# A two-layer transformer kernel: the Linear layer's products grouped by row count, LN2's steps of batch 0 placed half a unit earlier, the first sides' fills on ScalarE

## Chip, cores, metric

One NeuronCore of a Trainium2 chip. The metric is the time of one execution on the device in microseconds (us), taken as the median of several runs; lower is better. The engines are named PE (TensorE), DVE (VectorE), ACT (ScalarE), POOL (GpSimd) and SP (SyncE, which issues the transfers).

## What is computed

x has 2 batches of 1024 tokens with 128 features. Four sublayers follow one another, each on the layer-normalised x and added to x:

```
x = x + _L0_attn_ref(_layernorm(x), ...)   # causal attention, 16 heads of 64, scores/8, softmax/8
x = x + _L0_ffn_ref(_layernorm(x), ...)    # Linear layer with a gated low-rank part
x = x + _L1_attn_ref(_layernorm(x), ...)   # attention by squared distances, 16 heads of 8
x = x + _L1_ffn_ref(_layernorm(x), ...)    # 1 shared and 8 gated experts, 128 -> 512 -> 128, silu

# _L0_ffn_ref, the sublayer that the first part of the change touches
base = jnp.einsum('bcd,od->bco', x, W)
l = jnp.stack([... x @ Wd_i.T @ Wu_i.T for ranks 1, 2, 4, 8 ...], axis=2)
res = jnp.sum(ret[..., None] * l, axis=2)      # ret: the gate of the one chosen rank
return base + res

# _L1_attn_ref
Q = x @ W_k.T
scores = -(|q|^2 - 2 q.k + |k|^2) / sqrt(8)
attn_out = softmax(scores) @ Q @ merged, then @ W_o.T
```

All of it is in float32.

## The kernel before

The program is written engine by engine, and each engine runs its instructions in the written order. Semaphores join them; nothing is scheduled by a tool. All activations stay in SBUF: `x` and `xn` by token tiles of 128 (`[128, 16, 128]`), `xT` by features. PSUM is one tensor `banks` of eight banks of 512 columns.

**The first attention** runs in 16 units, u = 0 to 15, each one pair of heads of one batch (units 0 to 7 batch 0, 8 to 15 batch 1). `units0` calls `unit0_pe`, `unit0_act`, `unit0_dve` and `unit0_pool`. A unit has ten slots, handled two by two in five groups i = 0 to 4. In each slot PE makes a score block (`scores_pe`, L455 to L461), ACT takes its exp (`exp_act`, L603), POOL masks it where the diagonal is in it (L860) and adds it into `pacc` for the row sums (L868 for the first block of a half, L871 for the others), and PE multiplies it with the values (`pv_pe`, L481). In the same unit PE and DVE prepare the next one (n = u + 1): max products (`max_pe`, L406), row maxima by DVE (`max_dve`, L726 and L731), projections (L339) and their rounded and residual parts (ACT L608, DVE L710). `sums_pe` (L489) sums the rows of `pacc`, ACT takes logarithm and exp (L632, L634), DVE makes a Newton step (`newton_dve`, L739, L741) and `z_dve` (L752), and `out_pe` (L500) projects unit u - 1, which `xacc_dve` (L758) adds to x.

**Later sublayers of batch 0 are fitted into units 8 to 15**, by `if u == ...` lines in these functions: LN1 in units 8 to 10, the router in 11 and 12, in unit 13 at i = 1 the Linear layer (`linear_mid_pe`, L1127 base product with 128 rows, L1128 low-rank product with 16 rows, eight tiles of each in two halves, one bank for a half; `x_mid_dve`, L1135, adds it to x). LN2 follows: `stats_mid_dve` (L948) at i = 3 of unit 13, `aggr_mid_dve` (L952) and `eps_mid_dve` (L956) at i = 4, `rstd_mid_act` (L961, L963) at i = 4, `newton_mid` (L969 to L975) on POOL at slot 0 of unit 14, `norm_mid_dve` (L980, eight tiles) at i = 0 of unit 14, and at i = 1 PE's transposes (`turn_mid_pe`, L992), which wait for the normalised tiles and for the third maximum of n = 15, because they reuse its banks. Maxima, normalising and all else on DVE are in one queue.

**In unit 15** the first of the eight units of the second attention is set up: `heads1_pe` (L1200), `merged_pe`, `proj1_pe` and `norm1_pe` (L1211, L1217) at i = 0 and 1, into banks 6 and 7. From them `sides1_dve` makes the two matrices of the distance product: for each half of 512 columns a rounded copy (L1243), two fills (L1246) and two additions (L1250). `s_rl` counts the last two kinds. `out_pe` of unit 14 at i = 3 of unit 15 uses bank 7 and waits for `s_rl` 8, that is for all sides. `merged_wo_pe` (L1168) at i = 4 uses bank 6 and waits for `s_rl` 4. DVE's `newton_dve(u, 0)` and `xacc_dve(u - 1)` stand at i = 3.

**The second attention** (`attn1_pe`, and the same for the other engines) has 8 units of 32 blocks: a distance product (L1278), exp on ACT (`exp1_act`, L1305), products with the values (L1292). The Linear layer of batch 1 is fitted into its third unit, in four parts of two tiles. The experts come last.

## Time and profile before

| | |
|---|---|
| three runs | 1069.88, 1070.07, 1075.11 us |
| median | 1070.07 us |
| the profiled execution, its own time | 1073.41 us |
| its span, first to last instruction | 1071.7 us |
| its mean granted PE clock | 0.971 of full |
| first attention, with its start | to about 557 us |
| second attention | about 557 to 820 us |
| experts, with the last layer norm and router | about 820 us to the end |

The page gives busy time by engine and the largest groups of instructions; the timeline gives instructions in order of time, merged where they are alike, with the idle time before them and what ended it. An fp32 matmul appears as two instructions. Starts and waits are exact; the ends of matmuls are modelled, so durations of stages are read here from start to start.

### The profile page before, as it was taken

The numbers are of one execution on the slowest core, as the hardware profiler recorded it, in microseconds if no ns is written. First come the engines' busy times: TensorE is split into PE (matmuls) and PEld (weight loads), VectorE is DVE, ScalarE is ACT, GpSimd is POOL, SyncE is SP. The second block draws the span as 40 slices with busy tenths as digits, with TensorE's granted clock in tenths as the row PEclk, the third lists the DMA queues.
The fourth block names the chain that finished last, engine by engine and source line by source line (L and its number), as shares of the span: only waits on it lengthen the run. The fifth ranks groups of instructions, "written<-read, shape, count | busy, mean of one in ns | idle before, by whom it ended". The sixth has DMA issues, their size and how long they took to land.

```text
span 1071.7 us, 18837 instructions
## 1 busy us (share of the span) xinstructions
PE 1002.6 (94%) x6927; PEld 591.6 (55%) x6927; DVE 718.7 (67%) x1481; ACT 698.5 (65%) x1019; POOL 561.5 (52%) x504
## 2 busy tenths in 40 slices
PE   4789999999999999998989999999996599999997
PEld 3546666666666666665643333333222377877785
DVE  5767777777778768757555434434212699999998
ACT  3346666666566666635548998899996576666564
POOL 3267877787777768844860000000000258887885
PEclk9699999999999999988999999999999699999999
DMA  2000000000000000200000010000000003121201
GB/s 96 8 9 8 1 9 9 8 9 9 9 9 10 1 9 9 59 1 1 2 3 7 9 14 10 11 10 9 13 11 11 1 2 120 71 87 59 78 40 39
DMA packets 24927, 23.52 MB, mean 22 GB/s; under 512 B 17612, under 2 KB 20316, under 8 KB 23820
## 3 DMA queue, kind: packets, MB, share of 16 engines
q1 hardware_dynamic: 24844, 22.42, 7.4%
q8 instruction: 52, 0.85, 0.3%
q14 instruction: 31, 0.25, 0.1%
HBM read 19.20 MB, written 1.11 MB: 19 GB/s over the span
## 4 chain that ended last, share of the span: by engine, by line
PE 65%; DVE 20%; issue 9%; ACT 3%; SPq 1%; DMA 1%; DVEq 0%; ACTq 0%
PE banks L481 11%; PE banks L1292 10%; PE banks L1278 6%; DVE big L1699 5%; PE banks L339 4%; PE banks L406 4%; PE banks L455 4%; PE banks L500 3%; PE banks L461 3%; PE banks L489 3%; PE banks L459 3%; PE banks L457 3%; PE banks L432 3%; ACT prob L603 1%; PE banks L1211 1%
## 5 line engine op out<-in xcount | busy, mean ns | idle before, releaser
L871 POOL TENSOR_TENSOR pacc<-pacc,prob 128x1024 f32<-128x1024 f32 (+3 forms) x160 | 274.8, 1717 | 82.9 <-ACT prob L603 71.4
L1305 ACT ACTIVATE prob<-banks 128x1024 f32<-128x1024 f32 x256 | 240.4, 1068 | 20.8 <-PE banks L1278 19.5
L603 ACT ACTIVATE prob<-banks 128x1024 f32<-128x1024 f32 (+1 forms) x160 | 150.1, 940 | 150.0 <-PE banks L461 145.4
L1732 POOL TENSOR_TENSOR big<-prob,big 128x512 fp32r<-128x512 f32 x108 | 165.1, 1549 | 59.3 <-ACT big L1682 32.5
L481 PE MATMUL banks<-prob,v 128*64 128x512 f32 (+3 forms) x768 | 146.3, 503 | 0.0
L1688 ACT ACTIVATE prob<-banks,w 128x512 f32<-128x512 f32 x144 | 94.4, 685 | 70.9 <-PE banks L1650 70.8
L1292 PE MATMUL banks<-prob,v 128*32 128x512 f32 x1024 | 136.2, 604 | 1.2 <-DVE pacc L1313 1.0
L1225 POOL TENSOR_TENSOR wqkv<-wqkv 64x512 f32<-64x512 f32 x8 | 8.3, 1033 | 197.9 <-DVE wqkv L1221 197.9
L1670 PE MATMUL banks<-big 128*128 128x512 f32 x432 | 106.6, 392 | 4.5 <-POOL big L1732 4.5
L1650 PE MATMUL banks<-big 128*128 128x512 f32 x432 | 106.2, 394 | 1.3 <-ACT prob L1688 1.3
L1278 PE MATMUL banks<-big 32*128 32x512 f32 x512 | 100.8, 503 | 0.8 <-ACT prob L1305 0.8
L726 DVE TENSOR_REDUCE mxa<-banks 128x2 f32<-128x1024 f32 x64 | 77.0, 1222 | 31.7 <-PE banks L406 31.0
L1278 PEld LDWEIGHTS banks<-big 32*128 32x128 f32 x512 | 43.2, 181 | 94.6 <-ACT prob L1305 61.3
L1670 PEld LDWEIGHTS banks<-big 128*128 128x128 f32 x432 | 80.2, 188 | 24.7 <-POOL big L1732 5.6
L1650 PEld LDWEIGHTS banks<-big 128*128 128x128 f32 x432 | 81.8, 190 | 20.0 <-ACT prob L1688 2.1
L731 DVE CUSTOM_DVE_ANT_0 banks<-banks,msk,mxa 128x128 f32<-128x128 f32 (+3 forms) x128 | 65.7, 556 | 39.0 <-PE banks L406 38.3
L860 POOL TENSOR_SCALAR_AFFINE_SELECT prob<-prob 128x256 f32<-128x256 f32 x128 | 50.6, 408 | 74.2 <-ACT prob L603 74.1
L731 DVE CUSTOM_DVE_ANT_0 banks<-banks,msk 128x256 f32<-128x256 f32 (+3 forms) x128 | 59.8, 520 | 35.0 <-PE banks L406 35.0
L481 PEld LDWEIGHTS banks<-prob,v 128*64 128x64 f32 x768 | 50.4, 139 | 57.4 <-issue 44.5
L406 PE MATMUL banks<-big 64*128 64x512 f32 (+3 forms) x384 | 70.9, 395 | 9.6 <-DVE big L710 3.2
L455 PE MATMUL banks<-big 64*128 64x512 f32 (+3 forms) x384 | 74.2, 383 | 0.0
L461 PE MATMUL banks<-big,onesr 64*128 64x512 f32 (+3 forms) x384 | 67.5, 346 | 0.0
(257 smaller groups left out, 1671.8 us busy)
## 6 DMA issues: line engine op xcount, KB each, us to landing
prob<-gate_rows SPq DMA_DIRECT2D x8, 1024.0 KB, 4.6
w<-in_experts SPq DMA_DIRECT2D x9, 514.0 KB, 3.6
wqkv<-in_wqkv SPq DMA_DIRECT2D x16, 193.0 KB, 2.4
x<-in_x SPq DMA_DIRECT2D x4, 256.0 KB, 4.7
zz<-pacc SPq DMA_DIRECT2D x64, 16.0 KB
wpr<-pacc SPq DMA_DIRECT2D x64, 16.0 KB
out<-x SPq DMA_DIRECT2D x4, 256.0 KB, 2.3
wpr<-in_wpr SPq DMA_DIRECT2D x1, 512.0 KB, 5.7
```

Source lines behind the costliest of these rows:

```text
L406: mm = pe.matmul(banks[:, bank + h, at:at + width(s, c)], qh[HP[h], w, s * P:(s + 1) * P], kh[HP[h], w, c * BLK:c * BLK + width(s, c)], st ...
L455: pe.matmul(banks[:, bank + h, at:at + wd], kh[HP[h], w, k], qh[HP[h], w, q], start=True, stop=False)
L481: mm = pe.matmul(banks[HP[h], 4 + half, o:BLK], v[:, w, t, HP[h]], pr[:, g % NRING, h, at:at + wd], start=(t == 0), stop=(t == (2, 7)[half]))
L603: act.activation(pr[:, g % NRING, :, 0:wd], banks[:, 2 * (j % 2):2 * (j % 2) + 2, 0:wd], ACT.Exp, scale=SCALE0).then_inc(s_exp, 1)
L731: ins = dve.tensor_tensor_reduce(out=sc, in0=sc, in1=msk[:, BLK - wd:BLK], scale=1.0, scalar=low, op0=ALU.add, op1=ALU.max, accum_out=mx[: ...
L871: pool.tensor_tensor(pacc[:, half, :, o:BLK], pacc[:, half, :, o:BLK], p_[:, :, at:at + wd], ALU.add).then_inc(s_padd, 1)
L1278: mm = pe.matmul(banks[:, 2 * pair1(n) + k, :], l1[hr, w, t * P:(t + 1) * P], r1[hr, w, sbk * BLK:(sbk + 1) * BLK], start=True, stop=True)
L1292: mm = pe.matmul(banks[32 * h:32 * h + 32, 6, :], qv[:, u % 2, t, h, :], prob[:, prob1(2 * m + h // 2), h % 2 * BLK:(h % 2 + 1) * BLK], st ...
L1305: act.activation(prob[:, prob1(n), :], banks[:, 2 * pair1(n):2 * pair1(n) + 2, :].rearrange("p b c -> p (b c)"), ACT.Exp, scale=2 * SCALE1 ...
L1650: mm = pe.matmul(banks[:, i % 3, :], w2[:, w, a_, i * P:(i + 1) * P], x2[:, b_, c], start=(j == 0), stop=(j == 2))
L1670: mm = pe.matmul(banks[:, 4 + tb, :], w2[:, w, a_, wd], act2[b_][:, tb % 2, i, :], start=(i == 0 and a_ == 0 and b_ == 0), stop=(i == NI - ...
L1732: pool.tensor_tensor(act2[1][:, tb % 2, i, :], hid[:, tb % 2, i, :], act2[0][:, tb % 2, i, :], ALU.subtract).then_inc(s_hlP, 1)
```

## The change

It has three parts, and the arithmetic is the same sum for every output, apart from the order in which PSUM is written in the first.

1. `linear_mid_pe` issues the base products of a part first and then its low-rank products. `start` is set on the part's first tile of a bank alone, `stop` on the last low-rank one.
2. LN2 of batch 0: aggregation and epsilon at i = 3 of unit 13, directly behind the statistics; `rstd_mid_act` at i = 3; `newton_mid` on POOL before slot 9 of unit 13; tiles 0 to 3 normalised at i = 4 of unit 13, tiles 4 to 7 at i = 0 of unit 14.
3. Unit 15: ACT makes the fills (`fill1_act`, the first half behind the logarithms at i = 1, the second behind the exps at i = 2). DVE makes both rounded copies first and then the four additions (`sides0_dve`). The additions of slots 4, 5 and 6 into `pacc` go from POOL to DVE (`padd_dve`), at i = 2. `out_pe`, `xacc_dve` and the statistics of unit 14 go from i = 3 to i = 4.

```diff
@@ unit0_pe
-                    if not first:
+                    if not first and not last:
                         out_pe(pe, u - 1, 7)
@@
                     elif last:
                         merged_wo_pe(pe)
+                        out_pe(pe, u - 1, 7)
@@ unit0_act
+                    elif last:
+                        fill1_act(act, 0)
                 elif i == 2:
+                    if last:
+                        fill1_act(act, 1)
@@
                     if u == 11:
                         router_norm_act(act, 0)
+                    elif u == 13:
+                        rstd_mid_act(act, 1, 0)
@@ unit0_dve
+        def padd_dve(dve, j):
+            u = 2 * PAIRS - 1
+            half, g, done = SLOTS[j][0], NS * u + j, 12 * u + ADDED[j] - 1
+            dve.wait_ge(s_exp, g + 1)
+            dve.wait_ge(s_padd, done)
+            dve.tensor_tensor(pacc[:, half, :, :], pacc[:, half, :, :], pr[:, g % NRING, :, :], ALU.add).then_inc(s_padd, 1)
@@
                     elif u == 14:
-                        norm_mid_dve(dve, 1, 0)
+                        norm_mid_dve(dve, 1, 0, range(4, TB))
@@
                     elif last:
-                        sides1_dve(dve, 0, 0, 6)
-                        sides1_dve(dve, 0, 1, 7)
+                        sides0_dve(dve)
@@
+                elif i == 2 and last:
+                    for j in LAST_DVE:
+                        padd_dve(dve, j)
@@ unit0_pool
-                elif u == 14 and j == 0:
+                elif u == 13 and j == 9:
                     newton_mid(pool, 1, 0)
@@
+                if last and j in LAST_DVE:
+                    continue
@@ linear_mid_pe
             for t in part:
                 c = b * SEQ + half * BLK + t * P
-                to = banks[:, bank, t * P:(t + 1) * P]
-                pe.matmul(to, xT[:, c:c + P], wbase[:, :], start=True, stop=False)
-                mm = pe.matmul(to, hgT[b][half][:, t * P:(t + 1) * P], wup[:, :], start=False, stop=True)
+                pe.matmul(banks[:, bank, t * P:(t + 1) * P], xT[:, c:c + P], wbase[:, :], start=(t == 0), stop=False)
+            for t in part:
+                mm = pe.matmul(banks[:, bank, t * P:(t + 1) * P], hgT[b][half][:, t * P:(t + 1) * P], wup[:, :], start=False, stop=(t == 3))
@@ new
+        def fill1_act(act, hf):
+            cc, c = cst[:, C_COL:C_COL + 6], slice(hf * BLK, (hf + 1) * BLK)
+            act.wait_ge(s_hi, hf + 1)
+            for k, t in enumerate((r1, l1)):
+                act.activation(t[:, 0, c], hi1[:, 0, c], ACT.Identity, bias=cc[:, 3 * k + 2:3 * k + 3], scale=cc[:, 3 * k + 1:3 * k + 2]).then_inc(s_fill, 1)
+
+        def sides0_dve(dve):
+            cc = cst[:, C_COL:C_COL + 6]
+            for hf in range(2):
+                dve.wait_ge(s_nm, hf + 1)
+                dve.tensor_copy(hi1[:, 0, hf * BLK:(hf + 1) * BLK], banks[:, 6 + hf, :]).then_inc(s_hi, 1)
+            for hf in range(2):
+                c = slice(hf * BLK, (hf + 1) * BLK)
+                for k, t in enumerate((r1, l1)):
+                    dve.wait_ge(s_fill, 2 * hf + k + 1)
+                    dve.scalar_tensor_tensor(out=t[:, 0, c], in0=banks[:, 6 + hf, :], scalar=cc[:, 3 * k:3 * k + 1], in1=t[:, 0, c],
+                                             op0=ALU.mult, op1=ALU.add).then_inc(s_rl, 2)
```

PE in unit 13, group 1, between the row sums and the value products, before (`wbase` marks the base product, `wup` the low-rank one; a row is one matmul of the program, 16 in all, of which the first eight are here):

```order
L489 MATMUL banks<-pacc,ones 64x512 x2
L1127 MATMUL banks<-wbase,xT 128x128
L1128 MATMUL banks<-wup,prob 128x128
L1127 MATMUL banks<-wbase,xT 128x128
L1128 MATMUL banks<-wup,prob 128x128
L1127 MATMUL banks<-wbase,xT 128x128
L1128 MATMUL banks<-wup,prob 128x128
L1127 MATMUL banks<-wbase,xT 128x128
L1128 MATMUL banks<-wup,prob 128x128
```

and after:

```order
L489 MATMUL banks<-pacc,ones 64x512 x2
L1148 MATMUL banks<-wbase,xT 128x128 x4
L1150 MATMUL banks<-wup,prob 128x128 x4
L1148 MATMUL banks<-wbase,xT 128x128 x4
L1150 MATMUL banks<-wup,prob 128x128 x4
L481 MATMUL banks<-prob,v 64x512 x2
```

The alternation of the two kinds has become four runs of four.

DVE from the end of unit 13 to group 0 of unit 14, before (`mxa`, `mx` are the row maxima, `mv` the aggregated statistics, `xn` the normalised tiles):

```order
700 L710 SCALAR_TENSOR_TENSOR big<-banks,wqkv,big 128x512 x2
701 L952 BN_AGGR mv<-st 128x2 x9
702 L956 TENSOR_SCALAR rs<-mv 128x8
703 L731 ISA banks,mx<-banks,msk 128x256
...
715 L710 SCALAR_TENSOR_TENSOR big<-banks,wqkv,big 128x512 x2
716 L980 TENSOR_SCALAR xn<-x,mv,rs 128x128 x8
717 L731 ISA banks,mx<-banks,msk 128x512
```

and after:

```order
691 L974 BN_AGGR mv<-st 128x2 x8
692 L978 TENSOR_SCALAR rs<-mv 128x8
693 L736 ISA banks,mx<-banks,msk,mxa 128x256
...
702 L715 SCALAR_TENSOR_TENSOR big<-banks,wqkv,big 128x512 x2
703 L974 BN_AGGR mv<-st 128x2
704 L1002 TENSOR_SCALAR xn<-x,mv,rs 128x128 x4
705 L736 ISA banks,mx<-banks,msk 128x256
...
717 L715 SCALAR_TENSOR_TENSOR big<-banks,wqkv,big 128x512 x2
718 L1002 TENSOR_SCALAR xn<-x,mv,rs 128x128 x4
719 L736 ISA banks,mx<-banks,msk 128x512
```

Eight aggregations and the epsilon stand before the last maxima of unit 13, and the eight normalisations have become four and four.

DVE in unit 15 from group 1 on, before (L1243 rounded copies, L1246 fills, L1250 additions of the sides; L739, L741 Newton step):

```order
755 L1243 CAST big<-banks 128x512
756 L1246 TENSOR_SCALAR big<-big,cst 128x512 x2
757 L1250 SCALAR_TENSOR_TENSOR big<-banks,cst,big 128x512 x2
758 L1243 CAST big<-banks 128x512
759 L1246 TENSOR_SCALAR big<-big,cst 128x512 x2
760 L1250 SCALAR_TENSOR_TENSOR big<-banks,cst,big 128x512 x2
761 L739 TENSOR_TENSOR banks<-banks,rall 128x512
762 L741 SCALAR_TENSOR_TENSOR banks<-banks,rall 128x512
763 L758 SCALAR_TENSOR_TENSOR x<-banks,x 128x128
764 L948 BN_STATS st<-x 128x6
765 L752 TENSOR_TENSOR zz<-zr0,banks 64x256 x4
```

and after:

```order
757 L1285 CAST big<-banks 128x512 x2
758 L1290 SCALAR_TENSOR_TENSOR big<-banks,cst,big 128x512 x4
759 L785 TENSOR_TENSOR pacc<-pacc,prob 128x1024 x3
760 L744 TENSOR_TENSOR banks<-banks,rall 128x512
761 L746 SCALAR_TENSOR_TENSOR banks<-banks,rall 128x512
762 L757 TENSOR_TENSOR zz<-zr0,banks 64x256 x4
763 L763 SCALAR_TENSOR_TENSOR x<-banks,x 128x128
764 L970 BN_STATS st<-x 128x6
```

The four fills have left DVE, three additions of POOL's have come, and `xacc_dve` stands behind `z_dve`.

## Rows read from the trace of the kernel before

**Rows 1.** The page's first view: busy us, share of the span, instructions.

```profile
PE 1002.6 (94%) x6927; PEld 591.6 (55%) x6927; DVE 718.7 (67%) x1481; ACT 698.5 (65%) x1019; POOL 561.5 (52%) x504
```

**Rows 2.** Waits of PE, whole span: us in total, times, longest us.

```profile
PE banks L992 <- DVE mx L731: 3.5, 1, 3.5
...
PE banks L500 <- DVE big L1250: 2.5, 1, 2.5
```

**Rows 3.** Timeline of PE, unit 13: start us, us, instruction, [idle before <- releaser].

```profile
455.23 0.49 PE L1127 MATMUL banks<-wbase,xT 128*128 128x128 f32 x2
455.65 0.48 PE L1128 MATMUL banks<-wup,prob 16*128 16x128 f32 x2
...
463.95 3.68 PE L481 MATMUL banks<-prob,v 128*64 128x512 f32 x12
...
469.39 0.39 PE L406 MATMUL banks<-big 64*128 64x512 f32 x2
```

**Rows 4.** Stretches: us, PE busy (instructions), granted clock, DMA share, GB/s.

```profile
455.00:459.00 4.00, 4.00 (x21) 1.00 0.00 0
459.00:469.00 10.00, 10.00 (x33) 0.50 0.00 0
...
500.00:506.50 6.50, 5.72 (x22) 0.50 0.00 0
```

**Rows 5.** PE's timeline in unit 14, and the weight loads of line L1148 (ns min/median/max).

```profile
522.28 2.05 PE L1148 MATMUL banks<-wkT,xT 128*128 128x128 f32 x16
524.17 0.27 PE L418 MATMUL banks<-cst,mx 128*68 128x128 f32 x1
...
L1148 PEld LDWEIGHTS banks<-wkT,xT x32: 186/192/192, 522.3 to 693.4; 128*128 128x128 f32 x32
```

**Rows 6.** Timeline of PE, unit 10, the same place in the unit.

```profile
360.34 1.09 PE L992 MATMUL banks<-cst,xn 128*128 128x128 f32 x8
361.36 1.94 PE L481 MATMUL banks<-prob,v 128*64 128x512 f32 x12
...
364.27 0.40 PE L406 MATMUL banks<-big 64*128 64x512 f32 x2
```

**Rows 7.** Timeline of DVE, units 13 and 14.

```profile
482.84 0.49 DVE L731 CUSTOM_DVE_ANT_0 banks<-banks,msk,mxa 128x256 f32<-128x256 f32 x1 [1.21 <-PE banks L406]
...
488.17 0.70 DVE L952 BATCH_NORM_AGGREGATE mv<-st 128x2 f32<-128x6 f32 x9
...
491.12 0.30 DVE L731 CUSTOM_DVE_ANT_0 banks<-banks,msk 128x128 f32<-128x128 f32 x1 [1.22 <-PE banks L406]
...
494.09 5.23 DVE L980 TENSOR_SCALAR xn<-x,mv,rs 128x128 f32<-128x128 f32 x8
```

**Rows 8.** Timeline of DVE in the second attention: batch 1's LN2, POOL idle.

```profile
666.23 2.14 DVE L980 TENSOR_SCALAR xn<-x,mv,rs 128x128 f32<-128x128 f32 x8
```

**Rows 9.** Timeline of PE, unit 14.

```profile
500.78 1.94 PE L992 MATMUL banks<-cst,xn 128*128 128x128 f32 x8 [3.49 <-DVE mx L731]
...
507.57 0.39 PE L406 MATMUL banks<-big 64*128 64x512 f32 x2
```

**Rows 10.** Timelines of PE, DVE, ACT and POOL, unit 15.

```profile
549.40 2.22 PE L500 MATMUL banks<-wpr,zz 128*64 128x128 f32 x32 [2.46 <-DVE big L1250]
...
543.80 4.13 DVE L1246 TENSOR_SCALAR big<-big,cst 128x512 fp32r<-128x512 f32 x2
...
541.66 1.95 ACT L603 ACTIVATE prob<-banks 128x1024 f32<-128x1024 f32 x2 [4.79 <-PE banks L461]
...
542.77 7.40 POOL L871 TENSOR_TENSOR pacc<-pacc,prob 128x1024 f32<-128x1024 f32 x3 [5.49 <-ACT prob L603]
```

**Rows 11.** ACT's line L634 (ns min/median/max), and a group of DVE's (busy us, mean ns).

```profile
L634 ACT ACTIVATE rall<-rall x16: 631/632/635, 70.6 to 547.6; 128x512 f32<-128x512 f32 x16
...
L1635 DVE TENSOR_TENSOR big<-w,big 128x1024 fp32r<-128x1024 f32 x8 | 9.8, 1226 | 0.3
```

**Rows 12.** Timeline of ACT, second attention, behind a part of the Linear layer.

```profile
650.04 1.94 ACT L1305 ACTIVATE prob<-banks 128x1024 f32<-128x1024 f32 x2 [0.97 <-PE banks L1278]
```

More of the change, by code:

```diff
@@ L224, in build_kernel @@
             "merged_done", "merged_masked", "merged_wo_done", "merged_wo_stored", "qtm_done", "qtm_stored"))
-        s_pj, s_pf, s_qc, s_sq, s_nm, s_hi, s_rl, s_qv = (sem(n) for n in (
-            "q_projected", "sides_projected", "q_copied", "q_squared", "norms_done", "q_rounded", "sides_filled", "qv_filled"))
+        s_pj, s_pf, s_qc, s_sq, s_nm, s_hi, s_rl, s_qv, s_fill = (sem(n) for n in (
+            "q_projected", "sides_projected", "q_copied", "q_squared", "norms_done", "q_rounded", "sides_filled", "qv_filled", "sides_begun"))
         s_st1, s_exp1, s_pv1, s_zs, s_ln1, s_rz, s_zn, s_op1, s_x1 = (sem(n) for n in (
@@ L696, in unit0_act @@
                         mrow_act(act, n, x_, 0, 2)
-                    if u == 13:
-                        rstd_mid_act(act, 1, 0)
-                    elif u == 14:
+                    if u == 14:
                         qtm_store_mid(act, 0, 0, 6)
@@ L771, in attn0_dve @@
             units0(dve, unit0_dve)
+        LAST_DVE = (4, 5, 6)
+        def padd_dve(dve, j):
[4 more added lines that the diff above has]
+            dve.tensor_tensor(pacc[:, half, :, :], pacc[:, half, :, :], pr[:, g % NRING, :, :], ALU.add).then_inc(s_padd, 1)
         def unit0_dve(dve, u, w, bu, bn, first, last):
@@ L803, in unit0_dve @@
                     elif last:
-                        sides1_dve(dve, 0, 0, 6)
-                        sides1_dve(dve, 0, 1, 7)
+                        sides0_dve(dve)
                 elif i == 2 and first:
                     router_const_dve(dve, 1)
+                elif i == 2 and last:
+                    for j in LAST_DVE:
+                        padd_dve(dve, j)
                 elif i == 3:
                     newton_dve(dve, u, 0)
-                    if not first:
+                    if not first and not last:
                         xacc_dve(dve, u - 1, 7)
@@ L819, in unit0_dve @@
                             stats_mid_dve(dve, 1, k)
+                        for k in range(TB):
+                            aggr_mid_dve(dve, 1, k)
+                        eps_mid_dve(dve, 1, 0)
                 elif i == 4:
@@ L823, in unit0_dve @@
                         lo_dve(dve, n + 1, w, 1)
+                    if last:
+                        xacc_dve(dve, u - 1, 7)
+                        stats_mid_dve(dve, 0, u - 1)
                     if not first:
@@ L830, in unit0_dve @@
                     elif u == 13:
-                        for k in range(TB):
-                            aggr_mid_dve(dve, 1, k)
-                        eps_mid_dve(dve, 1, 0)
+                        norm_mid_dve(dve, 1, 0, range(4))
         def unit0_pool(pool, u, w, bu, bn, first, last):
@@ L975, in newton_mid, with norm_mid_dve @@
             e.tensor_tensor(r3, r3, r0, ALU.mult).then_inc(s["newton"], 1)
-        def norm_mid_dve(dve, k, b):
+        def norm_mid_dve(dve, k, b, part=range(TB)):
             dve.wait_ge(lb[k]["newton"], 4 * b + 4)
-            for n in range(b * TB, (b + 1) * TB):
+            for n in (b * TB + t for t in part):
                 dve.tensor_scalar(xn[:, n, :], x[:, n, :], mv[:, n, 0:1], rs[:, 3, n:n + 1], ALU.subtract, ALU.mult).then_inc(lb[k]["norm"], 1)
```

## Prediction

> **What bounds the kernel now.** I read the page first: TensorE (PE) is busy 94% of the span [rows 1], and in the first attention it runs almost without gaps, so a microsecond helps only if PE gets it. The other engines' idle time there ends with PE's results. Then the table of waits for PE: in the part that the diff touches it holds two large ones, 3.5 us before the transposes L992 (unit 14) and 2.5 us before the output projection L500 (unit 15) [rows 2]. Then PE's timeline around the Linear layer's products of batch 0 (unit 13) and the granted clock by stretches. The 32 instructions of this stage (each fp32 matmul is two) take 463.95 - 455.23 = 8.72 us [rows 3], and the clock, at full level (2.4 GHz) from 455 to 459, is at half (1.2 GHz) from 459 to 469. It is at half again from 500 to 506.5, after the 3.49 us in which PE stood still [rows 4]. So PE loses time here in three ways: slow small products, two waits, two stretches at half clock.
>
> **Part A, the Linear layer of batch 0.** Before, each base product (128 rows) is followed by a low-rank one (16 rows). Two instructions take 455.65 - 455.23 = 0.42 us at full clock [rows 3]. Nothing in the trace shows this stage grouped; the nearest row is L1148, sixteen instructions of the base product's shape in a row: 524.17 - 522.28 = 1.89 us, 0.236 us a pair [rows 5]. I take the difference, 0.182 us, as the price of each change of row count. Before there are 16 changes (with the entry), after it 4, so the stage should take 16 x 0.236 + 4 x 0.182 = 4.50 us at full clock, a gain of 4.22. Bounds: if the changes cost nothing in grouped form 3.8 us; if the row count is not the cause (next products wait for something else), 16 x 0.42 = 6.7 us at best, and 8.72 with the clock as now.
>
> The stretch behind it, up to the first max product of unit 13's second group, takes 469.39 - 463.95 = 5.44 us at half clock [rows 3]. Unit 10 has the same instructions at full clock: 364.27 - 361.36 = 2.91 us [rows 6]. If the shorter, denser stage keeps the clock up, 2.53 us come back here. Whether it does is open: L1148's two microseconds at the same density kept the clock, the present stage at 0.209 us an instruction lost it. I take "kept", since 4.5 us end soon after the 3.8 us that the present stage runs at full clock.
>
> The weight loads bear on this. In L1148's run a load takes 192 ns [rows 5] but the products start 118 ns apart, so loads are hidden under products of the same rows. The Trainium skill, "TensorE: Matmul & The Clock Gate", "What overlaps and what doesn't", says that weight loads overlap running matmuls only when the row group differs. By that, grouping would buy nothing, and the sum would lack part A's 4.22 and part D; this trace disagrees with it.
>
> **Part B, LN2 of batch 0 half a unit ahead.** In unit 14 VectorE (DVE) normalises eight tiles in one piece, 5.23 us [rows 7], before the maxima that PE's transposes wait for. The same eight tiles take 2.14 us where GpSimd (POOL) is idle [rows 8]. The change puts four of them behind unit 13's last step and four in the old place. It also moves eight aggregations and the epsilon (nine aggregations take 0.70 us at 488.17 [rows 7], eight and the epsilon 0.79; I take 0.87 with the gaps) into a gap of 1.21 us in unit 13 [rows 7]: they fit. DVE's path to the maxima: it is free at 488.3. Then come X (four tiles) and the first maximum, 0.87 (it ran from 488.17 + 0.87 to the idle time that began at 491.12 - 1.22 = 489.90 [rows 7]). The second maximum and two splits take 494.09 - 491.12 = 2.97, then Y (four tiles), then the third maximum, 1.4 (500.78 less the end of the eight tiles, 499.32, [rows 7, 9]). The second maximum cannot start before 491.12 by PE, so the end is 493.5 + max(X, 1.95) + Y. X and Y are 1.07 each with POOL idle, 2.6 each at today's rate; I take 2.2, as POOL adds at both places. That gives about 497.9, and PE is there at 500.78 - 3.49 = 497.29 [rows 9]. With 0.15 us to pass it on PE waits 0.8 us, where it waited 3.49: a gain of 2.7 (1.9 at 2.6 each, 3.5 with no contention). What else moves: ScalarE's (ACT) two small instructions (I estimate 0.2 us each, on eight columns, from DVE's aggregation) come before unit 13's exp of slot 8, which PE releases just then: at most 0.4 us for ACT, which idles again right after. POOL's four Newton steps, on eight columns as well and about 1 us by the same estimate, now stand before slot 9's mask; behind them are the mask and two adds, and the value products that need the mask come 4 us later. Neither reaches PE.
>
> A wait of under 1 us should not cost the clock. From the transposes' start to the next max product before: 507.57 - 500.78 = 6.79 us [rows 9]; the same in unit 10: 364.27 - 360.34 = 3.93 [rows 6]. Gain 2.86.
>
> **Part C, the last unit.** PE waits 2.46 us before L500 for the last of the sides [rows 2, 10]. The cause is that two fills took 4.13 us on DVE [rows 10] while POOL made three adds of 2.4 to 2.5 us [rows 10]. The fills go to ACT: at 0.63 us each (the nearest row, ACT's exp on 128x512 in SBUF [rows 11]) the first two fit into ACT's 4.79 us of idle time [rows 10], the exp behind them starts 0.5 us later. The other two follow that pair of exps, about 544.0 to 545.2. DVE then has its last side at about 546.0 instead of 549.3, just before L500 starts at 549.40 [rows 10]. The three adds follow on DVE, 1.23 us each by the nearest row of this size with both inputs in SBUF [rows 11], against 2.47 on POOL: 549.6, where the sums' Newton step, due right behind the sides now, starts at about 549.2: 0.4 us late, with nobody waiting soon. L500 now stands behind unit 15's last scores and the product with W_o, at about 550.9, when all sides are long there. So the wait goes; the work is the same. The gain is 2.46, with 2.0 and 2.5 as bounds, since exp 6 comes 0.6 us later and scores 8 need it only 2 us after that. POOL, with three adds fewer, ends before the row sums need it.
>
> **Part D, the Linear layer of batch 1.** In the second attention it runs in four parts of two tiles, with four changes of row count each, two after it: 8 x 0.182 = 1.46 us. ACT idles about 0.97 us behind each part because PE is late [rows 12], so PE sets the pace and all of it counts. Bounds 0 and 1.5.
>
> **The sum** is 4.22 + 2.53 + 2.7 + 2.86 + 2.46 + 1.46 = 16.2 us. Against the profiled execution's own 1073.41 us this gives 1057.2. The median of the three runs is 3.34 us lower, 1070.07. The time outside the span is the same kind in both, so something in the profiled execution was slower; a half-clock stretch like part B's (2.86 us) is about that size. If the median run lacks it, the median loses 13.4 and gives 1056.7. Both ways lead to about 1057; if the median has all of it, 1053.8.
>
> **Rivals.**
> R1, the clock falls in the grouped stage as well: 0.7 us of it at half clock (+0.7) and the stretch behind as now (+2.5): about 1060.3. For it: the present stage loses it with no idle time at all. Against: L1148's run.
> R2, the row count is not what costs, the edit does not do what it says: +4.22, +1.46, and +2.53 as the clock falls: 1065.2. For it: both kinds of product follow each other into the same PSUM addresses now, which L1148's do not. Against: L1148 itself, which shows the faster pace for this shape. The Trainium skill's sentence above on weight loads would lead to this case too.
> R3, DVE's two halves are both held up by POOL at worst: X and Y of 3.3 put the maximum at 500.1, PE waits 3.0 us and the clock falls: +2.2, and +2.86: 1061 to 1062.
> R4, slower than before, one mechanism: PE's clock. Grouped small products, the transposes of unit 14 and L500 behind the W_o product leave PE sparse at new moments; if the clock then stays at half through unit 14, about 38 us, this costs 19 us and gives 1076. It decides above 27 us of added half clock, since a microsecond at half clock costs 0.5 and the gain is 13.4. Against: every half-clock stretch now ends within 10 us [rows 3, 4].
> R5, more than forecast: the median holds every term, 1053.8.
>
> **Chances.** Forecast (1055 to 1059) 0.46, R1 0.16, R2 0.12, R3 0.12, R4 0.04, R5 0.10. To hold 8 in 10 the range runs from 1052.5 (R5 with its bounds) to 1063.5 (past R1 and R3); R2 and R4 are left out. A measurement here can tell 0.5%, 5.35 us: below 1064.7 is faster. That holds in all but R4 and the larger part of R2: faster 0.85, same 0.10, slower 0.05.
>
> **What the profile after would show.** A right: the sixteen products in about 4.5 us, pairs at 0.24 inside a group, and no half clock around them. A wrong: pairs still at 0.42 (R2), or half clock behind (R1). B right: PE's wait before the transposes under 1.5 us and full clock behind; wrong: DVE's normalisations over 3 us in each half. C right: no wait before L500, fills on ACT at 0.6 us; wrong: PE waits for exp 6, for the W_o product's bank or for POOL's last adds. D right: each part 0.36 us shorter and ACT's gap smaller by as much; wrong: ACT's gap gone and PE waiting for exps. A new wait of PE over 2 us anywhere would make the forecast wrong.

## Result

The changed kernel takes 1057.57 us (median of 4 runs, 1056.38 to 1058.85), the kernel before 1071.53 (median of 4). The ratio on record is 0.9848, 95% interval 0.9824 to 0.9873: 1.5% faster. The ratios on record are not the quotients of the medians given beside them; here that quotient is 0.9870, which lies inside the interval. The forecast was about 1057. In the experiments below the kernel before had medians of 1073.94 (26 runs) and 1074.12 (11) on one chip and 1073.13 (11) on another, and the changed kernel once more 1058.58 (5 runs), ratio 0.9862 (0.9839 to 0.9884).

The profiled execution of the changed kernel took 1056.50 us with a span of 1054.8, against 1073.41 and 1071.7. The difference of the spans, 16.9 us, lies where the change is. PE's timeline in unit 13 (columns as in [rows 3]; L1148 is the base product, L1150 the low-rank one, the last row the max product that [rows 3] ends with):

```profile
454.97 1.16 PE L1148 MATMUL banks<-wbase,xT 128*128 128x128 f32 x8
456.06 1.15 PE L1150 MATMUL banks<-wup,prob 16*128 16x128 f32 x8
457.15 1.16 PE L1148 MATMUL banks<-wbase,xT 128*128 128x128 f32 x8
458.23 1.15 PE L1150 MATMUL banks<-wup,prob 16*128 16x128 f32 x8
459.32 1.94 PE L481 MATMUL banks<-prob,v 128*64 128x512 f32 x12
...
462.22 0.40 PE L406 MATMUL banks<-big 64*128 64x512 f32 x2
```

The stage takes 459.32 - 454.97 = 4.35 us where it took 8.72, the stretch behind it 2.90 where it took 5.44 [rows 3]. The clock by stretches (us, PE busy, granted clock, DMA share, GB/s), for the places of [rows 4]:

```profile
454.00:459.00 5.00, 5.00 (x36) 1.00 0.00 0
459.00:464.00 5.00, 4.94 (x36) 1.00 0.00 0
486.00:490.00 4.00, 4.00 (x36) 1.00 0.00 0
490.00:495.00 5.00, 5.00 (x38) 1.00 0.00 0
```

It is at full level in all four. PE in unit 14, the answer to [rows 9] (L1014 is the transposes' new line):

```profile
483.99 0.50 PE L339 MATMUL banks<-xhi,whl 128*128 128x512 f32 x1 [0.55 <-DVE mx L736]
...
490.20 1.09 PE L1014 MATMUL banks<-cst,xn 128*128 128x128 f32 x8
...
494.13 0.40 PE L406 MATMUL banks<-big 64*128 64x512 f32 x2
```

The wait of 3.49 us is gone and the transposes' stretch takes 3.93 us where it took 6.79. A wait of 0.55 us has come earlier in the unit. DVE and ACT around it, the answer to [rows 7]:

```profile
475.67 0.49 DVE L736 CUSTOM_DVE_ANT_0 banks<-banks,msk,mxa 128x256 f32<-128x256 f32 x1 [0.46 <-PE banks L406]
...
481.09 2.06 DVE L1002 TENSOR_SCALAR xn<-x,mv,rs 128x128 f32<-128x128 f32 x4
...
487.07 1.53 DVE L1002 TENSOR_SCALAR xn<-x,mv,rs 128x128 f32<-128x128 f32 x4
...
481.80 1.03 ACT L604 ACTIVATE prob<-banks 128x1024 f32<-128x1024 f32 x1 [1.47 <-POOL pacc L893]
```

The early aggregation fits: 0.46 us of the 1.21 us gap are left. Four tiles and four tiles are there, and ACT now waits 1.47 us for POOL, which has the Newton steps in front of slot 9. PE's wait of 0.55 us ends with maxima that stand on DVE right behind the first four tiles, which end at 483.07; the part on x7 settles that these four tiles are its cause.

The last unit, the answer to [rows 10]: PE, then ACT's fills (L1279), then DVE's last two additions of the sides (L1290):

```profile
532.80 1.08 PE L489 MATMUL banks<-pacc,ones 128*64 128x512 f32 x4 [0.30 <-ACT zr L627]
...
537.72 2.22 PE L500 MATMUL banks<-wpr,zz 128*64 128x128 f32 x32
...
527.42 1.53 ACT L1279 ACTIVATE big<-big,cst 128x512 fp32r<-128x512 f32 x2 [3.97 <-DVE big L1285]
...
530.66 1.52 ACT L1279 ACTIVATE big<-big,cst 128x512 fp32r<-128x512 f32 x2
...
531.57 1.46 DVE L1290 SCALAR_TENSOR_TENSOR big<-banks,cst,big 128x512 fp32r<-128x512 f32 x2 [1.76 <-ACT big L1279]
```

There is no wait before L500. One of 0.30 us has come before the row sums, because ACT stores the context only behind its second pair of fills.

Batch 1's Linear layer in the second attention, first base product and the value product behind the last part, before and after:

```profile
648.02 0.49 PE L1127 MATMUL banks<-wbase,xT 128*128 128x128 f32 x2
...
660.23 1.06 PE L1292 MATMUL banks<-prob,v 128*32 128x512 f32 x8
```

```profile
632.32 0.71 PE L1148 MATMUL banks<-wbase,xT 128*128 128x128 f32 x4
...
642.99 1.07 PE L1332 MATMUL banks<-prob,v 128*32 128x512 f32 x8
```

12.21 us have become 10.67. The whole account, from start to start in the two traces: 0.26 us before unit 13's stage, 4.37 the stage, 2.54 the stretch behind, 3.41 up to the transposes, 2.86 behind them, 2.3 in unit 15, 1.54 in batch 1; 17.3 us together, of which 0.4 are lost again after that.

### The profile page after: what moved, and what is told of

It reads as the page before. It is cut to its first block, busy times and chain, and to the rows that moved or that the text cites. A ratio compares the mean times of both kernels' runs of the same rounds, so it can differ in the third digit from the quotient of the medians.

```text
span 1054.8 us, 18841 instructions
## 1 busy us (share of the span) xinstructions
PE 991.7 (94%) x6927; PEld 586.4 (56%) x6927; DVE 716.0 (68%) x1480; ACT 702.4 (67%) x1023; POOL 554.9 (53%) x501
## 4 chain that ended last, share of the span: by engine, by line
PE 65%; DVE 19%; issue 10%; ACT 4%; SPq 1%; DMA 1%; DVEq 0%; ACTq 0%
PE banks L481 11%; PE banks L1332 11%; PE banks L1318 6%; DVE big L1739 6%; PE banks L339 5%; PE banks L406 4%; PE banks L455 4%; PE banks L500 3%; PE banks L489 3%; PE banks L461 3%; PE banks L459 3%; PE banks L457 3%; PE banks L432 3%; ACT prob L604 2%; PE banks L1233 1%
## 5 line engine op out<-in xcount | busy, mean ns | idle before, releaser
L893 POOL TENSOR_TENSOR pacc<-pacc,prob 128x1024 f32<-128x1024 f32 (+3 forms) x157 | 267.8, 1705 | 65.0 <-ACT prob L604 52.7
L481 PE MATMUL banks<-prob,v 128*64 128x512 f32 (+3 forms) x768 | 142.7, 493 | 0.0
L406 PE MATMUL banks<-big 64*128 64x512 f32 (+3 forms) x384 | 70.7, 394 | 9.0 <-DVE big L715 3.2
L461 PE MATMUL banks<-big,onesr 64*128 64x512 f32 (+3 forms) x384 | 67.2, 345 | 0.0
```

The costliest lines, as they stand in the source:

```text
L406: mm = pe.matmul(banks[:, bank + h, at:at + width(s, c)], qh[HP[h], w, s * P:(s + 1) * P], kh[HP[h], w, c * BLK:c * BLK + width(s, c)], st ...
L481: mm = pe.matmul(banks[HP[h], 4 + half, o:BLK], v[:, w, t, HP[h]], pr[:, g % NRING, h, at:at + wd], start=(t == 0), stop=(t == (2, 7)[half]))
L893: pool.tensor_tensor(pacc[:, half, :, o:BLK], pacc[:, half, :, o:BLK], p_[:, :, at:at + wd], ALU.add).then_inc(s_padd, 1)
```

## Experiments

Ratios are those on record, to the kernel before on the same chip. The last column is read from the one profiled execution of each kernel: from the start of PE's first turn of the maxima of unit 1 (L418, at 74 to 81 us), which no change touches, to the end of the span. It leaves out the start of the kernel, which varies (see the part on the prediction), but it is one execution each. For the kernel before it is 994.3, for the changed one 977.8.

| kernel | median, us | ratio (95%) | L418 to end, us |
|---|---|---|---|
| x1 grouping alone | 1066.43 | 0.9924 (0.9901 to 0.9946) | 986.4 |
| x2 LN2 alone | 1067.48 | 0.9948 (0.9932 to 0.9965) | 988.4 |
| x3 last unit alone | 1070.55 | 0.9978 (0.9961 to 0.9996) | 989.7 |
| x4 stage alternating, split in two | 1073.47 | 0.9988 (0.9972 to 1.0005) | 993.4 |
| x5 changed, low-rank one tile behind | 1062.96 | 0.9902 (0.9871 to 0.9932) | 979.1 |
| x6 before, all products of 128 rows (leaves out the low-rank part of batch 0) | 1066.39 | 0.9930 (0.9906 to 0.9954) | 987.5 |
| x7 changed, eight normalisations together | 1062.68 | 0.9899 (0.9868 to 0.9930) | 982.0 |
| x8 changed, adds on POOL | 1057.14 | 0.9843 (0.9808 to 0.9879) | 978.1 |
| x9 changed, fills on DVE | 1056.15 | 0.9846 (0.9817 to 0.9874) | 977.2 |
| x10 changed, L500 at its old place | 1057.04 | 0.9850 (0.9823 to 0.9878) | 977.5 |
| x11 changed, fewer changes of rows | 1057.48 | 0.9838 (0.9814 to 0.9862) | 977.0 |
| x12 the changed kernel again | 1058.58 | 0.9862 (0.9839 to 0.9884) | 977.5 |

### The three parts alone: x1, x2, x3

x1 is the kernel before with the change's edit to `linear_mid_pe` and nothing else.

```diff
-                pe.matmul(to, xT[:, c:c + P], wbase[:, :], start=True, stop=False)
-                mm = pe.matmul(to, hgT[b][half][:, t * P:(t + 1) * P], wup[:, :], start=False, stop=True)
+                pe.matmul(banks[:, bank, t * P:(t + 1) * P], xT[:, c:c + P], wbase[:, :], start=(t == 0), stop=False)
+            for t in part:
+                mm = pe.matmul(banks[:, bank, t * P:(t + 1) * P], hgT[b][half][:, t * P:(t + 1) * P], wup[:, :], start=False, stop=(t == 3))
```

> The kernel before with the grouped Linear products alone. If the change of row count costs and the dense stage keeps the clock: stage from 8.7 to about 4.4 us, the stretch behind it from 5.4 to 2.9, batch 1's four parts 1.5 us less in all; 8.4 us less than before, ratio 0.992. If the clock were kept by the other two parts of the change and not by the grouping: half clock behind the stage, 5.5 us less, ratio 0.995. PE's 3.5 us wait before unit 14's transposes stays in either case.

Its PE waits, and the clock over the grouped stage (458.25 to 462.59 in this execution):

```profile
PE banks L992 <- DVE mx L731: 3.5, 1, 3.5
```

```profile
458.00:463.00 5.00, 5.00 (x36) 1.00 0.00 0
```

The grouping alone keeps the clock; the old wait stays. 0.76% is 8.2 us, where 8.4 was expected; the medians differ by 7.5, the last column by 7.9.

x2 is the kernel before with the LN2 edits of the change alone.

```diff
+                        for k in range(TB):
+                            aggr_mid_dve(dve, 1, k)
+                        eps_mid_dve(dve, 1, 0)
...
-                        norm_mid_dve(dve, 1, 0)
+                        norm_mid_dve(dve, 1, 0, range(4, TB))
...
-                elif u == 14 and j == 0:
+                elif u == 13 and j == 9:
                     newton_mid(pool, 1, 0)
```

> The kernel before with LN2's moves alone. PE's wait before unit 14's transposes goes from 3.5 to under 0.5 us. If the half clock behind the transposes came from this wait: 6.3 us less in an execution that had it, ratio 0.994 to 0.997. If it came from somewhere else (the earlier half-clock stretch in unit 13), it stays, and 3.4 us are gained, ratio 0.997. The Linear stage stays at 8.7 us with half clock.

The clock behind the Linear stage of unit 13 in this kernel:

```profile
464.00:468.00 4.00, 4.00 (x22) 0.61 0.00 0
```

PE at the transposes, and at the output projection in unit 15, where the wait of the kernel before is still present:

```profile
495.82 1.09 PE L993 MATMUL banks<-cst,xn 128*128 128x128 f32 x8
...
541.57 3.33 PE L500 MATMUL banks<-wpr,zz 128*64 128x128 f32 x32 [2.47 <-DVE big L1251]
```

The transposes run without a wait, at full clock, though half clock was there behind the Linear stage in unit 13. So the half clock at the transposes came from their own wait. The second row shows something the kernel before did not show in its profile: L500 takes 3.33 us instead of 2.22, mostly at half clock, after a wait of the same 2.47 us. Five profiles have this wait: x2, x4 and x6 show half clock behind it, the kernel before and x1 do not. From L500's start to the W_o product the first three take 7.18, 7.23 and 7.12 us, the other two 5.63 and 5.64. So in such an execution the wait costs 1.5 us more than its own length, which part C's sum did not hold.

x3 is the kernel before with the last unit's edits alone.

```diff
-                        sides1_dve(dve, 0, 0, 6)
-                        sides1_dve(dve, 0, 1, 7)
+                        sides0_dve(dve)
...
                         merged_wo_pe(pe)
+                        out_pe(pe, u - 1, 7)
```

> The kernel before with the last unit's moves alone. The 2.5 us wait before the output projection goes, a wait of about 0.3 us before the row sums comes: 2.3 us less, ratio 0.998. If the other parts made room for it: a smaller gain, and PE waits for the fills on ScalarE.

0.22% is 2.4 us, with an interval from 0.4 to 4.2. PE around the transposes in this kernel, where part B's wait is as before:

```profile
500.07 1.06 PE L1013 MATMUL banks<-cst,xn 128*128 128x128 f32 x8 [3.49 <-DVE mx L736]
...
505.61 0.40 PE L406 MATMUL banks<-big 64*128 64x512 f32 x2
```

After the same wait the stretch takes 5.54 us here; it took 6.79 in the kernel before, and takes 3.93 at full clock. The wait brings half clock in both, but its price was 1.6 us in one and 2.9 in the other.

The three gains, 0.76 + 0.52 + 0.22 = 1.50%, add up to the whole change's 1.52%. The three intervals together leave 0.33% either way, so a help or hindrance among the parts of up to 3.5 us is not ruled out. The last column's gains, 7.9 + 5.9 + 4.6 = 18.4 against 16.5 us, do not settle it either, because half clock cost less in the profiles of x2 and x3 than in that of the kernel before: their Linear stages took 7.77 and 8.34 us, and x3's transposes are 1.25 us shorter.

### What makes the alternation slow: x5 and x6

x5 keeps the changes of row count and takes away that a product follows the one that wrote the same addresses; x6 does the reverse.

```diff
# x5, batch 0, on the changed kernel
+                for of, t in ((base, 0), (base, 1), (low, 0), (base, 2), (low, 1), (base, 3), (low, 2), (low, 3)):
+                    mm = of(t)
# x6, batch 0, on the kernel before
-                mm = pe.matmul(to, hgT[b][half][:, t * P:(t + 1) * P], wup[:, :], start=False, stop=True)
+                mm = pe.matmul(to, xT[:, c:c + P], wbase[:, :], start=False, stop=True)
```

> The changed kernel; in batch 0 each low-rank product stands one tile behind its base product (base 0, base 1, low 0, base 2, low 1, base 3, low 2, low 3 in each half). Six changes of row count in a half where grouping has two, but no product writes right behind the one that wrote the same addresses. If the row count costs: the stage takes 4.35 + 8 x 0.15 to 0.18 = 5.6 to 5.8 us at full clock. If writing into the same addresses costs: about 4.4 us.

> The kernel before; in batch 0 the low-rank product is replaced by the base product a second time, so the low-rank part of batch 0 is left out and the base part counted twice. Same number of products, same addresses in turn, but all with 128 rows. If the row count costs: the stage takes 32 x 0.118 = 3.8 to 4.0 us, and the clock stays at full. If writing into the same addresses costs: 0.209 us an instruction, 6.7 us or more, half clock as before.

PE's timeline of x5, the first run of two products, one single one, and the value products behind the stage:

```profile
458.25 0.71 PE L1146 MATMUL banks<-wbase,xT 128*128 128x128 f32 x4
458.90 0.48 PE L1148 MATMUL banks<-wup,prob 16*128 16x128 f32 x2
459.31 0.49 PE L1146 MATMUL banks<-wbase,xT 128*128 128x128 f32 x2
...
464.14 1.94 PE L481 MATMUL banks<-prob,v 128*64 128x512 f32 x12
```

and of x6, where L1127 and L1129 alternate on the same addresses:

```profile
454.64 0.49 PE L1127 MATMUL banks<-wbase,xT 128*128 128x128 f32 x2
454.97 0.39 PE L1129 MATMUL banks<-wbase,xT 128*128 128x128 f32 x2
455.19 0.39 PE L1127 MATMUL banks<-wbase,xT 128*128 128x128 f32 x2
...
458.41 1.94 PE L481 MATMUL banks<-prob,v 128*64 128x512 f32 x12
```

In x6 a product starts 0.22 us after the one before it on the same addresses, and the stage takes 3.77 us. In x5 a single product between two of other row count still takes 0.41 us, and the stage 5.89 us. The addresses are not the cause: R2's ground for doubt falls. The stage's time at full clock follows the number of changes: 16 changes 6.6 us (sixteen times 0.415, the pace of [rows 3]), 12 changes 5.89 (x5), 4 changes 4.35, 2 changes 3.96 (x11, below). From step to step that is 0.19, 0.19 and 0.20 us a change.

One rival is left by x5 and x6: base and low-rank product differ in their operands as well as in the row count, and each edit changes both together. The kernel before has rows that tell them apart, just ahead of the stage:

```profile
453.66 0.40 PE L461 MATMUL banks<-big,onesr 64*128 64x512 f32 x2
453.89 0.40 PE L406 MATMUL banks<-big 64*128 64x512 f32 x2
454.22 1.08 PE L489 MATMUL banks<-pacc,ones 128*64 128x512 f32 x4
```

From L461 to L406 both operands change and the 64 rows stay: 0.23 us for two instructions of 512 columns. From L406 to L489 the rows go from 64 to 128 as well: 0.33 us. So other operands alone cost nothing that these rows show, and a change of rows costs time in other products too, 0.10 us here. With this the row count is the cause.

### What brings the clock down in unit 13: x4

The kernel before, with the alternation kept and its two halves put apart:

```diff
                         linear_mid_pe(pe, 0, 0, 6)
-                        linear_mid_pe(pe, 0, 1, 7)
...
                     pv_pe(pe, u, w, 0, first)
                     pv_pe(pe, u, w, 1, first)
+                    if u == 13:
+                        linear_mid_pe(pe, 0, 1, 7)
```

> The kernel before; the Linear stage of batch 0 keeps its alternation, but its second half stands behind the value products of slots 0 and 1, so the sparse stretch is cut in two of 3.3 us with 2.9 us of dense work between. If a long sparse stretch brings the clock down: full clock throughout, both halves 3.35 us each, value products 2.9, about 4.5 us less than before, ratio 0.996. If the alternation by itself does it: half clock again, no gain, ratio 1.000.

The clock over the first half of the stage (458.05 to 461.38), behind it, and behind the second half:

```profile
458.00:461.00 3.00, 3.00 (x17) 1.00 0.00 0
461.00:464.50 3.50, 3.50 (x15) 0.59 0.00 0
...
468.00:471.50 3.50, 3.50 (x18) 0.56 0.00 0
```

Of the two expectations it was the second. The first half runs at full clock itself, and each is followed by half clock, so 3.3 us of the alternation were enough, and cutting it in two made two short half-clock stretches of one long one. Where the uncut stage alternates, its first row at half clock starts 3.7 us into it in the kernel before, 5.0 in x2 and 4.2 in x3. x5's 5.89 us with fewer changes, a longer stretch than any of these, had full clock throughout, in its one profile. So the length of the stage alone does not decide it. Why the alternating one loses the clock and x5's does not stays open.

### Normalising in one piece: x7

```diff
-                        norm_mid_dve(dve, 1, 0, range(4, TB))
+                        norm_mid_dve(dve, 1, 0)
...
-                        norm_mid_dve(dve, 1, 0, range(4))
```

(on the changed kernel; in `unit0_dve`, with the `elif` of the second).

> The changed kernel with all eight tiles normalised in one piece at the old place, the aggregation left early. If the split of the normalising is what removes PE's wait: the wait before unit 14's transposes is about 3 us (VectorE's early aggregation only lengthens its idle time before the second maximum), with half clock behind it: 3 to 6 us slower than the changed kernel. If the early aggregation does it: no wait.

PE and DVE in unit 14:

```profile
489.96 1.94 PE L1012 MATMUL banks<-cst,xn 128*128 128x128 f32 x8 [3.24 <-DVE mx L736]
...
495.31 0.39 PE L406 MATMUL banks<-big 64*128 64x512 f32 x2
```

```profile
483.52 4.97 DVE L1000 TENSOR_SCALAR xn<-x,mv,rs 128x128 f32<-128x128 f32 x8
```

The wait is back (3.24 us) and with it half clock (5.35 us instead of 3.93): 4.7 us together. The medians differ by 5.1, the last column by 4.2. It is the split, over the idle time that DVE has before the second maximum, that removes the wait.

Two smaller waits of PE change as well. The 0.55 us before the next projection (L339) is there in all profiles with the split, x2 among them, and not in x7, although ACT waits 1.48 us for POOL in x7 too, before its exp at 478.88, as it does in the changed kernel. So this wait is the price of the first four tiles on DVE, not of the Newton steps on POOL. And the kernel before has PE wait 0.46 us for ACT before L406 at 490.53, as ACT's two instructions for LN2 stand before its exp there and wait for DVE's epsilon; in x7 and in the changed kernel this wait is gone. The early moves alone are thus worth 0.25 and 0.46 us.

### Which of the last unit's moves matters: x8, x9, x10

```diff
# x8
-        LAST_DVE = (4, 5, 6)
+        LAST_DVE = ()
# x9: no fill1_act; in sides0_dve, ahead of the two additions of each half
+                for k, t in enumerate((r1, l1)):
+                    dve.wait_ge(s_hi, hf + 1)
+                    dve.tensor_scalar(t[:, 0, c], hi1[:, 0, c], cc[:, 3 * k + 1:3 * k + 2], cc[:, 3 * k + 2:3 * k + 3], ALU.mult, ALU.add).then_inc(s_fill, 1)
# x10
-                    if not first and not last:
+                    if not first:
                         out_pe(pe, u - 1, 7)
...
                         merged_wo_pe(pe)
-                        out_pe(pe, u - 1, 7)
```

> The changed kernel with the adds of slots 4 to 6 back on GpSimd, fills on ScalarE. If only the fills mattered: same time. If GpSimd is late for the last row sums: it needs 7.4 us for three adds, ends 2 to 3 us after VectorE's version (about 547 where PE wants the sums at 544.7), PE waits about 2 us there: 2 us slower than the changed kernel.

> The changed kernel with the four fills on VectorE again (in its new order: both rounded copies first), GpSimd's three adds still on VectorE. If GpSimd's adds were what held the fills up: the fills take 0.54 us each now, the last side comes no later than with ScalarE, same time as the changed kernel. If fills on VectorE are slow by themselves: 2 us each, the last side over 3 us later, PE waits for it before the W_o product or the output projection, 1 to 2 us slower.

> The changed kernel with PE's output projection of unit 14 back at i = 3, in front of slots 4 and 5's value products. In the changed kernel VectorE's last side ends at 533.0 and PE has the row sums done at 533.7, so: no wait there, same time within 0.5 us. If the later place was needed: a wait of 1 us or more before the output projection.

x8's waits of PE in unit 15 and behind it, and POOL's three adds:

```profile
PE banks L489 <- POOL pacc L893: 0.8, 1, 0.8
```

```profile
530.45 7.43 POOL L893 TENSOR_TENSOR pacc<-pacc,prob 128x1024 f32<-128x1024 f32 x3 [6.08 <-ACT prob L604]
```

POOL is late as expected, but by 0.8 us and not by 2, and most of it is made up by the next output projection: from the value products behind L500 to the next output projection PE takes 558.42 - 540.28 = 18.14 us here and 557.68 - 539.76 = 17.92 in the changed kernel. The time is the same within what can be told.

x9's second pair of fills on DVE, with POOL idle:

```profile
530.55 0.99 DVE L1286 TENSOR_SCALAR big<-big,cst 128x512 fp32r<-128x512 f32 x2
```

It takes 0.99 us, in [rows 10] it took 4.13 on the same engine with POOL adding. So POOL's adds held the fills up, as the prediction had it. That has two cures: fills away from DVE (x8), or adds away from POOL (x9). Each gives the whole gain within what can be told, and the change does both. x10's output projection, right behind the row sums:

```profile
533.53 2.13 PE L500 MATMUL banks<-wpr,zz 128*64 128x128 f32 x32
```

It starts without a wait: once the sides are early its later place is not needed.

### Further in the same direction: x11 and x12

```diff
-                        linear_mid_pe(pe, 0, 0, 6)
-                        linear_mid_pe(pe, 0, 1, 7)
+                        for kind in ("base", "low"):
+                            linear_mid_pe(pe, 0, 0, 6, kind=(kind,))
+                            linear_mid_pe(pe, 0, 1, 7, kind=(kind,))
...
-                            linear_mid_pe(pe, 1, 0, 7, (2 * i - 20, 2 * i - 19))
+                            linear_mid_pe(pe, 1, 0, 7, kind=(("base", "low")[i - 10],))
...
-                    if last:
-                        fill1_act(act, 1)
                     z_act(act, u, 0)
+                    if last:
+                        fill1_act(act, 1)
```

> The changed kernel with two more steps in the same direction: in batch 0 all eight base products, then all eight low-rank ones (two changes of row count where there were four); in batch 1 the four base products of a half in one slot and its four low-rank ones in the next (four changes for eight); and in unit 15 ScalarE stores the context before its second pair of fills. At 0.14 us a change 0.3 + 0.6 us, and PE's 0.3 us wait before the row sums goes: 1.1 us less than the changed kernel, ratio to it 0.999, near what can be told. If the longer base run without change loses the clock: 3 us slower.

> The changed kernel itself, for comparison on the same chip: 0.985 of the kernel before, 1056 to 1060 us.

x11's stage:

```profile
457.21 2.05 PE L1150 MATMUL banks<-wbase,xT 128*128 128x128 f32 x16
...
461.17 1.94 PE L481 MATMUL banks<-prob,v 128*64 128x512 f32 x12
```

The stage falls by another 0.39 us to 3.96, at full clock. The 0.30 us wait before the first row sums is gone, but one of 0.8 us comes before the second ones, as ACT's later fills make DVE's adds and then POOL's later. Its ratio of 0.9838 and the changed kernel's 0.9862 on the same chip have intervals that overlap: no gain can be told from the times. Batch 1's part takes 10.30 us where it took 10.67, so 0.4 us less and not 0.6. From L418 to the end x11's profile takes 977.0 us against 977.8 and 977.5 in the changed kernel's two: 0.5 to 0.8 us less where 1.1 was expected, one or two executions each.

## Why the prediction was right, and where it was not

**Part A** held in both terms: 4.35 us for the stage where 4.50 was forecast, 2.90 behind it where 2.91 was, full clock. x5 and x6 confirm the cause, and sharpen the price: 0.19 us a change, not 0.182, over a base pace of 0.112 us an instruction, not 0.118. The counts of 16 and 4 changes are right, but not "with the entry": the row sums ahead of the stage have 128 rows like the first base product, and the last change is the one to the value products behind it. The sentence of the Trainium skill that the prediction names ("TensorE: Matmul & The Clock Gate", "What overlaps and what doesn't") has weight loads overlap running matmuls only when the row group differs. The trace disagrees again: in x6 products of the same 128 rows start 0.11 us apart while a load takes 0.19 us, so loads are hidden under products of the same rows. What I did not see is that the alternation costs the clock even in 3.3 us of it (x4); I had tied the loss to the 3.8 us run.

**Part B** gained 3.41 + 2.86 = 6.27 us where 2.7 + 2.86 were forecast. The too large term was X and Y: I took 2.2 each "as POOL adds at both places", and they ran from start to start in 483.07 - 481.09 = 1.98 and 488.53 - 487.07 = 1.46. So PE had no wait before the transposes, not 0.8 us. Two terms were put at nothing: the first four tiles cost PE 0.55 us at the next projection, and the early aggregation gave back the 0.46 us for which PE had waited for ACT. Together 3.49 + 0.46 - 0.55 = 3.40 us, which is the 3.41 measured from start to start. The Newton steps on POOL were free for PE, as forecast: ACT waits 1.5 us for POOL in the changed kernel and in x7, and x7's PE has no wait from it. "If the wait goes, the clock stays" is shown by x2 and, from the other side, by x7. "Gain 2.86" is one execution's price: x1 had 2.8 us, x3 and x4 1.6, x6 1.5 and x7 1.4.

**Part C** gained 2.3 us for 2.46, against an execution in which the wait did not cost the clock; where it does, 1.5 us more are gained (x2, x4, x6), and the prediction had no term for that. ACT's fills took 0.72 us each from start to start, not 0.63 (the row with ACT's exp was not near enough, as the fill has a bias and a scale column), and the 0.3 us wait comes from there. The mechanism, POOL's adds, is shown by x9. The prediction took the three moves together for what was needed; x8 to x10 show that one of the first two was enough, within what can be told.

**Part D** gained 1.54 us for 1.46, and PE did set the pace there.

**The step that failed** is the one from the profiled execution to the median. I took the 3.34 us by which it lay above 1070.07 for part B's half clock. The three-run median was itself low: over 26 runs the kernel before had 1073.94. The profiled execution, at 1073.41, was the typical one. Executions differ at the start. The first row here is the kernel before's, the second x5's, the third x7's, all PE's turn of the maxima of unit 1 (L418), which no change touches:

```profile
77.37 0.27 PE L418 MATMUL banks<-cst,mx 128*68 128x128 f32 x1
```

```profile
80.37 0.27 PE L418 MATMUL banks<-cst,mx 128*68 128x128 f32 x1
```

```profile
74.10 0.27 PE L418 MATMUL banks<-cst,mx 128*68 128x128 f32 x1
```

A spread of 6.3 us is there before 81 us. That this made the three runs' median low is likely, but not shown, since none of the three has a profile. The forecast came out right because the other way, the full sum of 16.2 against the profiled execution's own time, gave 1057.2 as well. That the first way gave the same 1057 was luck: a base 3.9 us too low and a gain 2.8 us under the full sum nearly cancel. The gain against the typical time was 1073.94 - 1057.57 = 16.4 us, and 1073.13 - 1058.58 = 14.6 in the second comparison, not 13.4.

Of the rivals, R1, R2, R3 and R4 did not come: no half clock at the places named, the row count does cost, X and Y stayed under 2.2, and no new half-clock stretch appeared. R5's condition, that the typical execution holds every term, came true, but its 1053.8 did not, as it was counted from the low median.

## What to carry to other kernels

Small products with different row counts that alternate on TensorE are worth sorting by row count: a change cost 0.19 us here, more than the 0.11 us that an instruction needs, and the alternation was followed by half clock for up to 10 us. Where a wait of PE comes from another engine's queue, look in that queue for idle time earlier on and split the step over it; moving a part was enough. Where two engines slow each other down, moving either one's work can be enough, as it was here, so try the single moves before all of them; and add up gains against the profiled execution's own time, since a median of three runs can be low by more than a part of the change is worth (3.9 us here, part C 2.3). Where the start varies, compare two profiles by the time from a row ahead of every change to the end of the span.

## What the runs showed of the hardware that was not expected

- TensorE's clock fell from 2.4 to 1.2 GHz behind 3.3 us in which it was never idle, but alternated small products of 128 and 16 rows (x4); it stayed up over 5.89 us of the same 32 instructions with 12 changes instead of 16 (x5, one profile).
- The wait of 3.2 to 3.5 us before the transposes was followed by half clock in all six profiles that have it (the kernel before, x1, x3, x4, x6, x7), at a price of 1.4 to 2.9 us. The wait of 2.46 to 2.48 us before L500 was followed by half clock in x2, x4 and x6 and not in the kernel before and x1; it cost 1.5 us where it was.
- The start of the kernel, up to 81 us, varied by 6.3 us between profiled executions of kernels that are alike there.
